# ScalarE instead of SyncE issues the scatter and gather of the attention output, in a four-layer graph network

## The reference, cut to what matters

```python
x = _layernorm(x + _L0_gnn_ref(x, adj, adj, L0_gnn_b))                      # edge layer
x = _layernorm(x + _L1_gnn_ref(x, L1_gnn_W, L1_gnn_a, L1_gnn_beta, adj))    # graph attention
x = _layernorm(x + _L2_gnn_ref(x, adj, L2_gnn_weight, L2_gnn_bias))         # graph convolution
x = _layernorm(x + _L3_gnn_ref(x, adj, Wq, bq, Wk, bk, Wv, bv))             # masked attention, 8 heads of 64

# the fourth layer
q, k, v = (x @ Wq + bq), (x @ Wk + bk), (x @ Wv + bv)       # reshaped to 8 heads
scores = einsum('bihd,bjhd->bhij', q, k) / sqrt(64) + mask
out = einsum('bhij,bjhd->bihd', softmax(scores), v)
```

## Time and profile before

| | |
|---|---|
| median of three runs | 2570.09 us |
| profiled execution, its own time | 2571.1 us |
| its span, first to last instruction | 2569.1 us |
| TensorE busy (matmul) | 2444.0 us, 95% |
| VectorE busy | 2276.0 us, 89% |
| ScalarE busy | 1305.8 us, 51% |
| GpSimd busy | 1448.6 us, 56% |
| DMA engines, mean share busy | 59% |

### The profile page before, as it was taken

One profiled execution on the slowest core, in us unless ns is written; L12 is line 12 of the kernel. 1 busy time (PEld: TensorE's weight loads), 2 busy tenths in 40 slices (PEclk: granted clock), 3 DMA queues, 4 the chain that ended last, 5 costly groups with the idle time before them and its releaser, 6 DMA issues.

```text
span 2569.1 us, 54851 instructions
## 1 busy us (share of the span) xinstructions
PE 2444.0 (95%) x15497; PEld 2075.1 (81%) x15497; DVE 2276.0 (89%) x6933; ACT 1305.8 (51%) x4104; POOL 1448.6 (56%) x1806
## 2 busy tenths in 40 slices
PE   3799999999999999999999999999999999999983
PEld 2588888888888888888888888888888888888872
DVE  5798999999999999999999999999999999999962
ACT  3354554555555555555555555555555555554531
POOL 4655655656556565565655656556555565555521
PEclk8899999999999999999999999999999999999986
DMA  4155665666665666566666566666666656656554
GB/s 128 38 128 132 140 139 133 141 140 137 139 139 135 142 143 137 133 143 136 141 138 140 135 139 145 136 136 142 136 140 137 142 134 136 143 138 135 127 119 91
DMA packets 1382908, 342.56 MB, mean 133 GB/s; under 512 B 1084880, under 2 KB 1347152, under 8 KB 1382864
## 3 DMA queue, kind: packets, MB, share of 16 engines
q1 hardware_dynamic: 1382864, 342.05, 58.6%
HBM read 174.13 MB, written 167.77 MB: 133 GB/s over the span
## 4 chain that ended last, share of the span: by engine, by line
PE 45%; DMA 20%; ACT 9%; issue 7%; SPq 7%; POOL 7%; DVE 5%; POOLq 0%; ACTq 0%; DVEq 0%
DMA probs_t<-pt_hbm 10%; PE rot L901 8%; DMA pt_hbm<-probs 8%; PE rot L903 7%; PE rot L902 7%; SPq L284 5%; PE rot L937 4%; PE score L937 4%; ACT probs L509 4%; PE rot L1003 3%; PE score L1015 3%; POOL e L424 2%; ACT x L607 2%; PE rot L940 2%; PE score L940 2%
## 5 line engine op out<-in xcount | busy, mean ns | idle before, releaser
L901 PE MATMUL rot<-w_hi,y_hi 128*128 128x512 f32 x1024 | 418.7, 409 | 1.3 <-DVE y_lo L814 0.8
L381 POOL TENSOR_TENSOR ve<-mv,eps_col 128x1 f32<-128x1 f32 (+1 forms) x448 | 82.8, 199 | 581.1 <-DVE mv L664 581.1
L903 PE MATMUL rot<-w_hi,y_lo 128*128 128x512 f32 x1024 | 405.2, 396 | 0.0
L902 PE MATMUL rot<-w_lo,y_hi 128*128 128x512 f32 x1024 | 401.9, 392 | 0.0
L509 ACT ACTIVATE probs<-score,sc_nmax 128x128 f32<-128x128 f32 x1024 | 363.9, 382 | 38.8 <-DVE sc_nmax L672 38.8
L406 POOL TENSOR_TENSOR x<-x,o_norm 128x512 f32<-128x512 f32 x128 | 167.2, 1307 | 194.9 <-DVE o_norm L722 194.9
L417 POOL TENSOR_TENSOR x2b<-x,bias 128x512 f32<-128x512 f32 x128 | 163.3, 1276 | 200.8 <-ACT e L562 199.9
L672 DVE CUSTOM_DVE_ANT_0 score<-score,mask 128x128 f32<-128x128 f32 x1024 | 260.9, 313 | 0.0
L694 DVE CUSTOM_DVE_ANT_0 dot_tmp<-x,u 128x512 bf16<-128x512 f32 x256 | 250.9, 1017 | 5.5 <-ACT x L616 5.3
L424 POOL TENSOR_SCALAR e<-e 128x512 f32<-128x512 f32 x128 | 249.2, 1947 | 8.0 <-ACT e L562 8.0
L386 POOL TENSOR_TENSOR rs<-ve,half_neg 128x1 f32<-128x1 f32 (+1 forms) x448 | 250.1, 573 | 0.5
(11 more groups left out here) (119 smaller groups left out, 7258.7 us busy)
## 6 DMA issues: line engine op xcount, KB each, us to landing
pt_hbm<-probs SPq DMA_DIRECT2D x512, 128.0 KB, 2.7
probs_t<-pt_hbm SPq DMA_DIRECT2D x128, 512.0 KB, 4.0
x_in<-in_x SPq DMA_DIRECT2D x128, 256.0 KB, 2.9
xt_hbm<-x_b SPq DMA_DIRECT2D x512, 64.0 KB, 2.2
xt_f<-xt_hbm SPq DMA_DIRECT2D x128, 256.0 KB, 2.8
ot_hbm<-o_t SPq DMA_DIRECT2D x512, 64.0 KB, 2.3
o_norm<-ot_hbm SPq DMA_DIRECT2D x128, 256.0 KB, 2.7
out_x<-x SPq DMA_DIRECT2D x128, 256.0 KB, 2.3
```

The source lines that it names most:

```text
L901: pe.matmul(outp, lh, rh, start=first, stop=False)
L902: pe.matmul(outp, lh, rl, start=False, stop=False)
L903: return pe.matmul(outp, ll, rh, start=False, stop=last)
```

## The change

The helpers `scatter` and `gather` get the issuing engine as an argument. SyncE keeps the probabilities and `x3_b`. The scatter of `o_t` moves to ScalarE, behind `att_t` and ahead of the first exponentials; the gather into `o_norm` moves to ScalarE behind the last exponentials. The wait of the scatter on `x4_done` of the slot before is now a wait of the gather.

```diff
+        def scatter(eng, hbm, blocks, landed):
+            for a in range(P // BLOCK):
+                rows = slice(a * BLOCK, (a + 1) * BLOCK)
+                eng.dma_start(hbm.rearrange("n (b r) p -> r (n b) p", r=BLOCK)[:, :, rows],
+                             blocks[rows, :].rearrange("r (m c) -> r m c", c=BLOCK)).then_inc(landed, 16)
+
+        def gather(eng, tiles, hbm, landed):
+            eng.dma_start(tiles, hbm.rearrange("n q p -> q n p")).then_inc(landed, 16)
...
@@ SyncE
-                if slot.on(L_PV):
-                    slot.wait(sp, x4_done, L_PV, 1)
-                    slot.wait(sp, o_t_done, L_PV)
-                    scatter(ot_hbm, o_t, ot_scattered)
-                    slot.wait(sp, ot_scattered, L_PV, each=SCATTER)
-                    gather(o_norm[:, :, :].rearrange("p g (c e) -> p (g c) e", e=P), ot_hbm, ot_in)
...
@@ ScalarE
                     act.activation(att_t[:, b2, :], att_bank[:, 0:P], ACT.Copy).then_inc(att_t_done, 1)
+                if slot.on(L_PV):
+                    slot.wait(act, o_t_done, L_PV)
+                    scatter(act, ot_hbm, o_t, ot_scattered)
...
                 if slot.on(L_QK):
                     exponentials(slot, 1).then_inc(score_exp, 1)
+                if slot.on(L_PV):
+                    slot.wait(act, x4_done, L_PV, 1)
+                    slot.wait(act, ot_scattered, L_PV, each=SCATTER)
+                    gather(act, o_norm[:, :, :].rearrange("p g (c e) -> p (g c) e", e=P), ot_hbm, ot_in)
```

More of the change, by code:

```diff
@@ L278, in load @@
                   .then_inc(x_loaded[buf], 16)
[L280 to L288, removed]
             def load_weight(n):
@@ L315, in emit @@
                     slot.wait(sp, probs_b_done, L_PV)
-                    scatter(pt_hbm, probs_b, pt_scattered)
+                    scatter(sp, pt_hbm, probs_b, pt_scattered)
                     slot.wait(sp, pt_scattered, L_PV, each=SCATTER)
-                    gather(probs_t[:, :, :, :].rearrange("p c t n -> p (c t) n"), pt_hbm, pt_in)
+                    gather(sp, probs_t[:, :, :, :].rearrange("p c t n -> p (c t) n"), pt_hbm, pt_in)
                 if slot.on(L_TR):
                     slot.wait(sp, x3_b_done, L_TR)
-                    scatter(xt_hbm, x3_b, xt_scattered)
+                    scatter(sp, xt_hbm, x3_b, xt_scattered)
                     slot.wait(sp, xt_scattered, L_TR, each=SCATTER)
-                    gather(xt_f[:, :, :], xt_hbm, xt_in)
+                    gather(sp, xt_f[:, :, :], xt_hbm, xt_in)
                 if slot.on(L_LOAD):
```

## The result

The changed kernel takes **2662.15 us** (median of four runs, 2661.08 to 2662.40) against 2570.16 us for the kernel before on the same chip: 1.0362 times as long, with a 95% interval of 1.0349 to 1.0375.

A forecast was written before the change was run, and what follows sets the result against it. The loop through ScalarE and SyncE was taken to bound store slots, TensorE plain ones. 60 store slots x 1.8 us, 59 plain x 0.15 and 1 for the drain gave 118 us: forecast 2690 us, range 2640 to 2745.

The forecast's parts named there:

- The bound: Store slots (every second slot, normalising and storing two graphs) follow a ScalarE-SyncE loop, 19.01 us; plain slots follow TensorE, 18.79.
- What is removed: SyncE loses four scatter issues (1.94 us) and the gather (0.38 us) per slot; worth 0 in both kinds of slot.
- The gather on ScalarE: One issue behind the exponentials, running while the last ones execute: 0, at most 0.38 us.
- The price of an issue: Four issues on ScalarE cost SyncE's 1.94 us; other prices gave 1.5 or 2.38 us for four.
- The start of the issue: Scatter begins at 1207.2, behind `att_t`, making the first exponential 1.8 us late; from the start of `x_hi`, +1.25.
- The transport to the store: In store slots the whole loop shifts, normalisation, stores, scatter, gather and line 1003: +1.8 us, from 1.25 to 2.43.
- Plain slots: Cover for `probs_t` is just used up; the nearer trouble is line 972: 0 to 0.4 us, taken as 0.15.
- The drain: Last few stores, where TensorE waits anyway; on ScalarE the scatter fits ahead of the exponentials: 1 us in all.
- Run-ahead: Rival: ScalarE's sequencer issues the scatter as soon as `o_t` is there, +0.6 us per slot: 2606, up to 2640; chance 0.05.
- A free issue: Rival: ScalarE's arithmetic is held by less than about 0.08 us per slot at the first exponential: 2570; chance 0.04.
- A gain for SyncE: Rival: emptying SyncE's queue lets `probs` leave 0.2 us sooner, store slots 18.79 us: 2558; chance 0.04.
- The collision: Rival: the gather of `o_norm` flies beside output stores or the scatter of `probs`, stretching it by 1.7 us: over 2745; chance 0.06.

The follow-up runs named there:

- `dummy` kernels with two and four issues: Kernel before plus two or four small DMAs per slot issued by ScalarE between `att_t` and the first exponential: 2584.62 us (two), 2673.34 us (four).
- `gather_only`: Changed kernel with the scatter of `o_t` given back to SyncE, only the gather of `o_norm` on ScalarE: 2568.35 us, 0.9998.
- `dummy4_ahead`: Kernel before plus four 4 KB DMAs per slot to a scratch tensor, issued by ScalarE between `att_t` and the first exponential: 2673.34 us, 1.0402.
- `scatter_only`: Changed kernel with the gather of `o_norm` given back to SyncE, only the scatter of `o_t` on ScalarE: 2662.79 us, 1.0379.
- `stores_act_moved`: Changed kernel with the two output stores issued by ScalarE behind `x1` instead of by SyncE: 2759.28 us, 1.0734.
- `dummy4_behind_last`: Kernel before plus four small DMAs per slot issued by ScalarE behind `x1`, their scratch tensor allocated last: 2614.76 us, 1.0189.

## Why the prediction was right, and where it was off

**The bound** was read rightly. Store slots ran at the pace of the loop through ScalarE and SyncE, and what held the exponentials came out in the slot nearly one for one (+1.54 at the exponentials, +1.39 in the slot), while plain slots kept the pace of TensorE. Of the 1.39 us 0.83 are idle time directly ahead of line 1004. The rest was passed a little sooner, at lines 973 and 989, where VectorE was late: it waited 51.4 us in all for `x1` (`x` of line 617; 5.3 before), and then TensorE for it and for `k_sb`. The prediction had placed such a stall inside the same sum. For this reason one of its signs came out at half: the wait of the weight loads of line 1004 rose by 51 us (61.5 to 112.6) and not by about 100. The two `dummy` kernels with two and four issues move the same slot in the same way.

**What is removed: 0.** `gather_only` shows it for the gather. For the scatter `dummy4_ahead` does, which holds the exponentials nearly as long and leaves everything on SyncE: the scatter of `probs` starts at 10.15 us of the plain slots there and at 10.13 in the changed kernel, and at 11.52 and 11.54 of the store slots. SyncE without the other scatter is not sooner. The rule of the Trainium skill that was weighed there ("Perfetto Trace Analysis", DMA Optimizations) did not apply, as its condition was not met.

**The gather on ScalarE: 0.** Confirmed: issued at 1215.39 while the exponentials ran, with no gap in front of any.

**The price of an issue.** SyncE's 1.94 us for the four was taken; ScalarE took 2.06 here. The choice among the three prices was right.

**The start of the issue** is the step that was mis-sized, and it carries most of the miss in the loop. The prediction had it at 1207.2, as `att_t` started, because a wait instruction at this place had started then. The first issue came 0.11 us behind the start of `x_hi`, and 0.42 ahead of `att_t` (1211.80, 1211.91 and 1212.33 in the rows above). A DMA issue passes an arithmetic instruction that is still queued; the wait instruction read in the earlier trace rows had not. From `x_hi` the sum is 0.11 + 2.06 + 0.12 (from the last issue's end to the exponential) = 2.29 us, less the 0.69 of before = +1.60, and `x_hi` itself stands 0.05 sooner in the slot: +1.55. This was the low end of the prediction, +1.25, with a longer issue and two small hand-overs. The Trainium skill's rule on the queue of 8 ("Advanced Engine Details and Errata", Engine Queue Depths) was dismissed too fully: the trace agrees with it for `att_t`, which was passed while it stood in the queue. It gives a depth and not what a wait holds back, and the prediction's use of it for `x_hi` the trace does not bear out: the wait of `x_hi` for TensorE held everything behind it until 1211.80. `o_t` was ready at 1211.21, as VectorE's time line has it:

```profile
1210.51 0.70 DVE L821 STREAM_TRANSPOSE o_t<-rot 128x512 f32<-128x512 f32 x1
```

**The transport to the store.** +1.8 was carried through unchanged; 0.15 us of it were hidden, since the output normalisation had been waiting for GpSimd's `out_shift` too. The term came out as 54 loop slots x 1.39 = 75 us, where 54 x 1.8 = 97 stood. Of these 22 us, 14 are the start of the issue (54 x 0.26) and 8 are this cover.

**Plain slots.** 0.15 predicted, 0.10 measured in the loop. The cover was there as read: the exponentials came 1.54 us later, the scatter and the gather of `probs` left only 0.51 and 0.53 later (9.62 to 10.13 and 14.00 to 14.53), and TensorE did not wait for `probs_t`. The place named for them is where something grew, the weight load ahead of the small matmul of line 972, now 973. Its wait in the kernel before and then in the changed one:

```profile
PEld s_bank L972 <- DVE s_col L694: 32.6, 5, 9.5
```

```profile
PEld s_bank L973 <- DVE s_col L695: 58.9, 101, 9.4
```

That is 0.27 us for each of the 96 new waits, on the weight load; most of it did not reach the matmuls, as the plain slot with 18.88 us of matmul in 18.88 shows. The small matmul itself takes 0.06 of the 0.10 us (0.11 to 0.17 in the mean of the plain slots); no run parts the rest.

**The slots outside of the loop** were not seen as a case of their own. The first eight took 10.7 us more, where the prediction's terms give 3 store slots x 1.8 + 5 plain ones x 0.15 = 6. And it falls otherwise: each of the first six took 1.3 to 2.2 us longer, whether it stores or not, the last two under 0.15. For the sixth, a plain one, the granted clock is the reason, 18.80 us at the full clock before and now

```profile
244.31:264.82 20.51, 20.51 (x121) 17.45 (x121) 16.22 (x51) 8.62 (x29) 7.31 (x12) 0.92 0.53 117
```

TensorE is never idle in it, but runs at 1.2 GHz for 3.4 us, after 2.9 us without work. In `scatter_only` that fall comes at 202.8 us instead, and there the fourth slot is long (21.89 us) and the sixth is not (18.92). For the other five the clock was full throughout. The scatter of `probs` in a plain one of them, in the changed kernel:

```profile
169.53 2.25 SPq L278 DMA_DIRECT2D pt_hbm<-probs  x4
175.28 0.38 SPq L282 DMA_DIRECT2D probs_t<-pt_hbm  x1
```

5.75 us lie between, where the same slot had 4.53 before (168.28 to 172.81) and the plain slot of the loop has 4.39 (1239.22 to 1243.61). `dummy4_ahead` has longer first slots too (170.5 us) and `gather_only` has not (155.3), so it belongs to the late exponentials; what collides there with the scatter of `probs` stays open. Outside of the loop 12.6 us were forecast in all (6 x 1.8, 5 x 0.15 and 1) and 11 measured; since they fell in other slots and one part was the clock, that agreement is luck.

**The drain**: 1 us predicted, 2 measured with all that lies behind the loop.

**The rivals.** Run-ahead was half true, as above; its time of 2606 would have needed an issue free of the wait of `x_hi`, which no run has. A free issue is refuted for four and for two; one has cover enough to cost nothing. A gain for SyncE is refuted. The collision did not occur in the changed kernel's loop (no store slot there beyond its sum), but `stores_act_moved` and `dummy4_behind_last` show that it is real one or two microseconds further on, at 2.4 and 1.1 us from the scatter's start to its gather, on either side of the 1.7 that was taken from the earlier trace rows.

No version run here beat the kernel before.

## What to carry to other kernels

A DMA issue is not free for the engine that issues it: count it as an instruction of 0.3 to 0.55 us in that engine's order and ask who stands behind it. A busy share of 51% says nothing about that, since what counts is whether the engine lies on the loop at this place; adding one, two and four small DMAs there measures the cover directly. And a store or issue that is moved off a loop lands on something else: look at what is issued and flies at the new moment, and at whose buffer comes free later. Where a variant is slower than its waits explain, look at the granted clock of single slots: a slot without any idle time took 20.4 instead of 18.9 us here.

## What the runs showed of the hardware that was not expected

- TensorE's granted clock fell to 1.2 GHz for 3.4 us at a time, 23 and 26 times in the loops of the two kernels in which the engine idled longest in the store slots (2.0 us), and never in the loops of the others. A fall cost some 1.5 us, partly in slots that had no idle time of their own.
- A DMA issue leaves while the arithmetic instruction ahead of it is still queued behind a running one (issue 1211.91, `att_t` 1212.33); a wait instruction at the same place started only with that instruction (1207.2 and 1207.22 before).
- Issues on a second queue stretch a scatter of small pieces on the first: its four issues took 3.50 us instead of 2.38 with only 16 KB moved by the other engine, and 3.71 us beside two stores of 256 KB; from the scatter's start to its gather 5.59 and 6.96 us instead of 4.53. With the small DMAs all of the growth is in the issuing.
- Where a small scratch tensor is allocated matters: ahead of `pt_hbm` the gather of 512 KB from it took 4.3 us, behind it 4.1, and the kernel 2634 us against 2615 (on two chips, on which the kernel before differs by 1.0). Why was not tested.
